# A twelve-layer decoder on one core: softmax sums on TensorE, masking and maximum in one Vector instruction, no copies of the rows

## What is computed

```python
score = jnp.einsum('nqhd,nkhd->nhqk', q, k)
score = jnp.where(mask == 0, jnp.float32(-1e+20), score)
attn = jax.nn.softmax(score / jnp.sqrt(jnp.float32(D)), axis=-1)
out = jnp.einsum('nhqk,nkhd->nqhd', attn, v).reshape(n, lq, H * D)
return out @ Wo.T + bo          # L1x; the others differ in mask, heads and scaling
```

## Time and profile before

| | us |
|---|---|
| median of 3 runs | 3718.55 (3714.80 to 3731.33) |
| the profiled execution, its own time | 3732.82 |
| its span | 3731.0, granted clock 0.905 on average |
| PE busy | 2976.7 (80%) |
| DVE busy | 2299.4 (62%) |
| ACT busy | 1749.1 (47%) |
| POOL busy | 747.6 (20%) |

### The profile page before, as it was taken

The page is one execution under the profiler, slowest core; times in us unless marked ns, Lnnn a source line. Parts: engine busy times, 40 slices in busy tenths (PEclk is TensorE's granted clock), DMA queues, the critical chain, the costliest instruction groups (busy, mean ns, idle before and its releaser), DMA issues. The chain is left out here.

```text
span 3731.0 us, 54776 instructions
## 1 busy us (share of the span) xinstructions
PE 2976.7 (80%) x18517; PEld 2127.6 (57%) x18517; DVE 2299.4 (62%) x5176; ACT 1749.1 (47%) x4238; POOL 747.6 (20%) x865
## 2 busy tenths in 40 slices
PE   6999999998776895676877654595799848888797
PEld 5777777776565583454554324244596435555485
DVE  6777667775566335776777786897311675555423
ACT  6666666665421222776677262403332325555121
POOL 2111111110101421354444000000110003333422
PEclk8999999999898997898899777798799979999799
DMA  3111111111002583000000000000696010000476
GB/s 119 43 46 38 35 35 49 43 35 40 18 1 77 178 294 130 1 1 15 16 7 1 26 0 0 3 0 12 235 343 221 23 49 13 24 24 12 159 257 212
DMA packets 109524, 264.81 MB, mean 71 GB/s; under 512 B 16928, under 2 KB 71456, under 8 KB 104384
## 3 DMA queue, kind: packets, MB, share of 16 engines
q1 hardware_dynamic: 92896, 229.01, 18.4%
q0 software_dynamic: 8688, 23.78, 1.7%
q10 hardware_dynamic: 7664, 8.51, 0.7%
HBM read 213.72 MB, written 47.54 MB: 70 GB/s over the span
## 5 line engine op out<-in xcount | busy, mean ns | idle before, releaser
L1296 POOL TENSOR_TENSOR L3x_p<-L3x_p,L3x_rsum 128x512 f32<-128x512 f32 x128 | 133.0, 1040 | 448.1 <-DVE L3x_rsum L1377 448.1
L3025 POOL TENSOR_TENSOR L0a_sum_sq<-L0a_sum_sq,L0a_sq 128x512 f32<-128x512 f32 x56 | 73.1, 1305 | 698.7 <-ACT L0a_sq L2944 698.7
L2847 ACT ACTIVATE L0a_ex<-bank,L0a_nb 128x128 f32<-128x128 f32 x512 | 145.2, 367 | 126.1 <-PE bank L2776 125.6
L3113 DVE TENSOR_TENSOR L0a_ru<-bank,L0a_um 128x512 f32<-128x512 f32 x128 | 88.2, 689 | 182.1 <-PE bank L2768 167.2
L3104 DVE SCALAR_TENSOR_TENSOR L0a_xf<-L0a_xc,L0a_conv,L0a_xf 128x256 f32<-128x256 f32 x432 | 178.7, 482 | 9.1 <-ACT L0a_xf L2909 7.7
L1358 DVE SCALAR_TENSOR_TENSOR L3x_s<-bank,L3x_bias 128x512 f32<-128x512 f32 x128 | 86.4, 681 | 134.3 <-PE bank L1136 134.3
L1986 PE MATMUL bank<-L2a_half,L2a_diag 128*128 128x512 f32 x328 | 144.1, 601 | 28.4 <-ACT L2a_diag L1969 28.4
L1296 POOL TENSOR_TENSOR L1x_p<-L1x_p,L1x_rsum 128x512 f32<-128x512 f32 x128 | 132.2, 1040 | 138.6 <-DVE L1x_rsum L1377 138.6
L1300 POOL TENSOR_TENSOR L1a_p<-L1a_p,L1a_rsum 128x128 f32<-128x128 f32 (+1 forms) x256 | 123.0, 506 | 137.7 <-DVE L1a_rsum L1377 135.6
L2690 PE MATMUL bank<-x_feat,L0a_wx 128*128 128x256 f32 x576 | 138.1, 391 | 4.1 <-ACT L0a_xc L2896 4.1
L2776 PE MATMUL bank<-L0a_ru,L0a_vm 128*128 128x512 f32 x256 | 137.6, 621 | 0.0
(11 more groups left out here) (727 smaller groups left out, 8215.8 us busy)
## 6 DMA issues: line engine op xcount, KB each, us to landing
L2f_wt<-in_L2f_w SPq DMA_DIRECT2D x23, 2180.0 KB, 10.2
L0f_wt<-in_L0f_w SPq DMA_DIRECT2D x39, 898.0 KB, 6.7
L3f_wt<-in_L3f_w SPq DMA_DIRECT2D x39, 768.0 KB, 5.0
L0a_wx<-in_L0a_wx SPq DMA_DIRECT2D x72, 256.0 KB, 3.1
L0a_wz<-in_L0a_wz SPq DMA_DIRECT2D x32, 512.0 KB, 4.1
context_keys_values<-L2f_zeros ACTq DMA_DIRECT2D x32, 256.0 KB, 4.9
L0f_xs<-rows_by_expert SPq DMA_DIRECT2D x39, 128.5 KB, 3.4
L3f_xs<-rows_by_expert SPq DMA_DIRECT2D x39, 128.5 KB, 2.8
```

The lines of the kernel that those rows point to most:

```text
L1296: last = nc.gpsimd.tensor_tensor(both, both, rsum[r % 2][:, i, :].unsqueeze(2).to_broadcast([P, S, NK]), ALU.mult)
L2847: last = a(ex[g % 3][:, j, b * P:(b + 1) * P], bank[:, at:at + P], ACT.Exp, bias=nb[r % 2][:, b, h:h + 1])
L3113: rv.empty(vec.tensor_tensor(ru[g % 2][:], bank[:].rearrange("p (j t) -> p j t", j=2), um[:].unsqueeze(1).to_broadcast([P, 2, T]), ALU.mult))
```

## The change

1. Twins (L1a, L1x): `exponent` has no running sum any more, `reciprocal` and the division of the probabilities are gone. `weigh` multiplies each transposed tile twice: by the values, and by `summing`, a constant of zeros and ones (128 x 32 for each twin), which gives the sum of the probabilities in every row of the head's features. The accumulator bank now holds the values' product in columns 0 to 255 and the sums in 256 to 511, for one half of the heads, two steps. Every two steps ACT copies the bank to `raw` (`half`), DVE inverts 128 x 256 of it (`inverse`), and POOL multiplies into cT.
2. Masked stages (L1x, L3x, L2x): scale, mask and maximum are one DVE call, `tensor_tensor_reduce`: out = (bank + bias) * -scale, with the running minimum as second output. For L1x two calls (one for each tile of 256), for L3x one of 512, for L2x one of 256. ACT then waits for this alone. L1a keeps its two operations.
3. xb and cb are gone from `softmax_attention`: the projections read `c.xT` and `c.ctxT`. The loop of one turn is gone. L2x keeps its copies.
4. Order, twins: `take_turned` on DVE comes right after the first `scale_mask` of a step; q is projected in step 0 and k in step 1; the output projection comes one step later on PE, and DVE's part of it at the end of that step.

```diff
-        UNITS = [[("k", 0)], [("q", 0)], [("v", 0)], [("v", 1)]]
+        UNITS = [[("q", 0)], [("k", 0)], [("v", 0)], [("v", 1)]]
...
-        xb = [sb(f"xb{i}", [P, KD, T]) for i in range(2)]
-        cb = [sb(f"cb{i}", [P, KD, T]) for i in range(2)] if kind != "latent" else xb
+        raw = [sb(f"raw{i}", [P, 2 * T]) for i in range(2)] if twins == 2 else None
+        summing = sb("summing", [P, 2, DS]) if twins == 2 else None
...
                 def weigh(u):
+                    if twins == 2 and u % 2 == 0 and u:
+                        pe.wait_ge(sig("raw"), u // 2)
...
                     for kt in range(KT):
+                        for of in range(twins):
                             for d in range(G):
...
-                                    at = 0 if causal and kt == 0 else P if causal else 0
-                                    out = acc[0][rows_out, tile * T + at:(tile + 1) * T]
+                                    at = P if causal and kt else 0
+                                    out = acc[0][rows_out, of * T + at:(of + 1) * T]
+                                    weights = summing[:, e, :] if of else weights
...
-                        if step == 0 and r:
+                        if step == twins - 1 and r:
                             output(r - 1)
...
+                def half(i):
+                    act.wait_ge(sig("weighted"), 2 * (i + 1))
+                    if i >= 2:
+                        act.wait_ge(sig("cT"), i - 1)
+                    nc.scalar.activation(raw[i % 2][:], acc[0][:], ACT.Copy).then_inc(sig("raw"), 1)
...
+                def inverse(i):
+                    dve.wait_ge(sig("raw"), i + 1)
+                    below = raw[i % 2][:, T:2 * T]
+                    vec.reciprocal(below, below).then_inc(sig("reciprocal"), 1)
...
+                    for i in range(2 * ROWS):
+                        pool.wait_ge(sig("reciprocal"), i + 1)
+                        if i >= 2:
+                            pool.wait_ge(sig("projected"), i // 2)
+                        nc.gpsimd.tensor_tensor(cT[:, i % 2, :], raw[i % 2][:, 0:T], raw[i % 2][:, T:2 * T], ALU.mult).then_inc(sig("cT"), 1)
...
-                            ins = vec.scalar_tensor_tensor(out=s[:], in0=bank[:, 0:W], scalar=scale,
-                                                           in1=bias[r % 2][:].rearrange("p t s -> p (t s)"), op0=ALU.mult, op1=ALU.add)
+                            ins = vec.tensor_tensor_reduce(out=s[:, at:at + nk], in0=bank[:, at:at + nk], in1=bias[r % 2][:, e, :],
+                                                           scale=-scale, scalar=3e38, op0=ALU.add, op1=ALU.min,
+                                                           accum_out=nmax[r % 2][:, i, e:e + 1])
...
                         if twins == 2:
                             if d == 0 and g < total:
                                 scale_mask(g)
+                            if d == 0 and u > LA:
+                                take_turned((u - LA) * G - 1)
                             if d < G - 1 and g < total:
                                 scale_mask(g + 1)
-                            if d == 1 and u > LA:
-                                take_turned((u - LA) * G - 1)
+                    if twins == 2 and d == G - 2 and u > LA + 2 and (u - LA) % 2 == 1:
+                        inverse((u - LA - 3) // 2)
+                    if twins == 2 and i == G - 1 and r >= 2:
+                        output(r - 2)
...
-                        if g < total:
+                    if causal and g < total:
                         maximum(g)
```

More of the change, by code:

```diff
@@ new lines, in weigh @@
+                                last = nc.tensor.matmul(out, weights, come_from, start=(e == 0 and kt == 0 and of == 0),
+                                                        stop=(e == twins - 1 and kt == KT - 1 and of == twins - 1))
+                    last.then_inc(sig("weighted"), 1)
+                for what, i in in_order:
+                    project(0, what, i)
+                for u in range(-1, steps + LA + 1):
+                    own = range((u - LA) * G, (u - LA + 1) * G) if LA <= u < steps + LA else []
+                    for j in own[:G // 2]:
+                        transposes(j)
+                    if u > LA:
+                        r, step = divmod(u - LA - 1, PER_ROW)
+                        if step == twins - 1 and r:
+                            output(r - 1)
+                        weigh(u - LA - 1)
+                    if 0 <= u < steps:
+                        for r, what, i in units_at(u):
+                            project(r, what, i)
+                    if u + 1 < steps:
+                        r, step = divmod(u + 1, PER_ROW)
+                        if step == 0:
+                            key = ("q", r, MQ // 2 - 1)
+                            pe.wait_ge(t_emptied(key), n_emptied[key])
+                            pe.wait_ge(sig("k_taken"), K_UNITS * (r + 1))
+                            if kind == "latent":
+                                pe.wait_ge(sig(f"kv{r % 2}"), 32 * (r // 2 + 1))
+                        scores(u + 1)
+                    for j in own[G // 2:]:
+                        transposes(j)
@@ L1453, in _ @@
-                    if kind == "latent":
-                        spread(ROWS - 1)
-                    output(ROWS - 1)
-            sig.clear()
-        sig.close()
+                        vec.tensor_tensor(y[:], proj, rowwise(bo), ALU.add).then_inc(sig("out_read"), 1)
+                        dve.wait_ge(sig("out_read"), r + 1)
+                    vec.tensor_tensor(xr, xr, y[:], ALU.add).then_inc(sig("added"), 1)
+                hide(0)
+                for what, i in in_order:
+                    if what == "k":
+                        project(0, i)
@@ L1461, in layer1_attn @@
+                if twins == 2:
+                    inverse(2 * ROWS - 1)
+                if kind == "latent":
+                    spread(ROWS - 1)
+                output(ROWS - 1)
+        sig.clear()
+    sig.close()
 def layer1_attn(c):
```

646 lines of the change are left out of this document (296 added, 350 removed).

## The result

The changed kernel takes 3675.98 us (median of 4 runs, 3673.24 to 3678.78) beside 3724.94 for the kernel before (median of 4); the ratio is 0.9854, with a 95% interval of 0.9829 to 0.9878. The profiled execution takes 3678.78, with a span of 3677.0, 54 us less than the profiled one of before. Forecast was 3686, 33 us less, in a range of 3650 to 3712.

A forecast was written before the change was run, and what follows sets the result against it. PE was taken as nearest the bound in L1a and L1x and bounding L3x, DVE's chain L2x. Terms of -7.5 (L1a), -14.2 (L1x), -3 (L2x), -8 (L3x) gave -33 us: 3686 as median, range 3650 to 3712.

The forecast's parts named there:

- The signs that were named: What would show the forecast: `weigh` and output times, row pitch in L1x, DVE load, PE idle time, stage lengths.
- Sums on PE: L1a and L1x: sum matmuls add to PE's time, +25.3 and +32.0 us.
- Waits for DVE's copy: L1a and L1x: PE's waits for DVE's late copy go by the new order, -29.8 and -37.4 us.
- The waits for cT: L1a and L1x: cT is made a step earlier than needed, so PE's waits go, -5.4 and -4.2 us.
- New waits: L1a and L1x: allowance for PE waiting on DVE behind its large reciprocals, +8 and +4 us.
- The end of a stage: L1a and L1x: nothing covers the last reciprocal and POOL's product, +2.4 us a stage.
- Clock: Twin stages: PE waits less before outputs, so its clock holds better, -7 us in L1a, -10 in L1x.
- Rival (b): Clock holds everywhere, L3x included (-12), and allowances aren't needed (-12): -57 us, 3662; chance 0.15.
- Fused call: L1x on DVE: mask and maximum in one call take 0.50 us, between 0.34 and 0.84; by itself pays nothing there.
- L3x fused: L3x: ACT's exponential, and its copies for PE behind it, start earlier, 0.5 us a row, -4 us.
- L2x fused: L2x: one maximum a row leaves DVE's in-order chain, 8 x 0.34 = -3 us.
- Copies: Removing row copies: ACT's xb no longer delays cT in L3x, -4 us; first projection, -1 in each twin stage.

The follow-up runs named there:

- e7: Changed kernel with the sum products made twice and accumulated: 3726.03 us, ratio to before 0.9998; L1a +20.4, L1x +27.5 us.
- e1: Kernel before with one line moved, DVE's copy right after a step's first scaling in the twin stages: 3703.01 us, ratio to before 0.9897.
- e8: Changed kernel with DVE's copy put back behind the second scaling: 3715.4 us, ratio to before 0.9957; L1a +23.7, L1x +15.4 us.
- e3: Changed kernel with ACT's copy of the accumulator moved ahead of two exponentials: 3676.54 us, ratio to before 0.983; L1x -11.9, L1a -0.8 us.
- e2: e6 plus mask and maximum fused in L1x, L3x and L2x; no sums on TensorE: 3653.26 us, ratio to before 0.9757.
- e6: e1 with the row copies removed, nothing fused: 3651.94 us, ratio to before 0.978.
- e4: Changed kernel with scale, mask and maximum as two DVE instructions again in L3x and L2x: 3714.32 us, ratio to before 0.9917; L3x 398.0 us.
- e5: Changed kernel with ACT's copies of the rows of x put back in L3x alone: 3696.17 us, ratio to before 0.9899; L3x 399.5 us.

## Why the prediction was right, and where its sum was not

The direction, the range and the mechanism hold: order takes PE's holes away, the sums eat a good part of that, and the clock comes back. The sum of the stages was 20 us short (-32.7 against -52.5), 15 of it in L3x. In the twin stages it was 4 short each, and part of that nearness is luck: PE's new waits cost 5 and 8 us more than allowed, the sums 5 and 4.5 less, and the clock gave back more. The signs that were named came so: `weigh` 1.87 us for 2.0, the output's matmuls 1.89 for 2, L1x's rows every 31.48 for 31, DVE in L1x 63% busy, PE's idle time there 28.7 us, a little under the 30 named, and stages of 233, 262, 52 and 371 us for 235, 266, 48 and 384. By its terms:

**Sums on PE**, +25.3 and +32.0, taken at the upper end as the instructions are certain. The second set of e7 costs 20.4 and 27.5: right in that nothing hides them, 5 too much in each. The mis-sized thing is the distance taken as the price, 1.00 us for a `weigh` of 16. In the changed kernel it is 1.87 for 32. In L1a the half-width products are the cheap part: four groups start at 1642.42 and the next instruction at 1643.86, 1.44 us for 32 where 1.58 was taken.

**Waits for DVE's copy**, -29.8 and -37.4. They are gone to 1.4 and nothing; e1 and e8 show that it is the order that does it. The waits for cT, -5.4 and -4.2, are gone in mid-stage too; in L1x they were 3.4 before. The reasoning on places in the queue was right for the new place. It was wrong for the old one, where I counted two scalings and a maximum, and e8 shows three.

**New waits**, +8 and +4, for a DVE that is late behind large reciprocals. This isn't what came. The reciprocal takes 1749 ns as forecast from the earlier trace rows (1742) and no PE wait follows it. What came is 12.7 and 12.2 us for ACT's copy of the accumulator, every second step, which the prediction had at nothing. The change has one bank for values and sums, so `weigh` must wait until ACT has read it, and the copy stood behind four exponentials in a queue whose wait was in plain sight in the diff (`pe.wait_ge(sig("raw"), ...)`). e3 gets it back in L1x. The end of a stage was right in kind: 3.4 us of wait for POOL's last product in each, 2.4 forecast; the product takes 728 ns, not the 613 of the earlier trace rows, and ACT's copy of the bank, 0.58, stands ahead of the chain and was left out.

**Clock**, -7 and -10 in the twin stages, none in L3x. From length and mean clock, low clock loses 289.2 x 0.12 = 34.7 us in L1a before and 278.0 x 0.09 = 25.0 after, in L1x 24.0 and 14.1, in L3x 20.5 and 7.8: -9.7, -9.9 and -12.8. These clocks are rounded to 0.01, which is 3 us of such a stage, and they count idle time too. By PE's busy time for the same instructions, the sums taken at e7's 21.1 and 27.0, it is -12.2, -15.5 and -12.1. So the twins' terms were somewhat small, and L3x's, put at nothing, was the step that failed. Rival (b) had it at -12 with a chance of 0.15, and the reason given against it was that L3x keeps a hole of 1.65 before its output. The hole that is kept is 1.38 us, and the clock falls behind none of the eight outputs.

**Fused call**, taken at 0.50 between 0.34 and 0.84. It is the lower bound, one call every 0.35 us. In the rows of before ACT's read of 193 ns follows an exponential; on DVE the read of 83 ns lies beside the next call. The Trainium skill, VectorE: DVE Perf Modes, section Two Vector instructions with no wait between them, calls such an op two instructions; for an op without a pointer scalar it holds the second, the read, only where its output starts in another quadrant than the last output did. All of these start in the same one, and the two records at 1900.28 agree. The same page of the Trainium skill, section Rules for kernel authors, advises against fusing chained DVE ops for speed. Here the trace disagrees: 0.70 us an item for two calls stand in place of 683 + 667 ns, and e2 against e6 shows 9.2 us of L1x by it. The prediction said that this pays nothing in L1x by itself, and that was false without the sums. PE's waits for DVE's copy and scalings, 3.9 and 2.7 us in e6, are gone in e2, its waits for ACT grow by some 2, and its busy time falls by 5.7. That the clock rose because the waits went is likely, but no run takes the two apart. In the changed kernel the call wasn't undone in L1x, so what it is worth there is open.

**L3x fused**, -4, measured 10.5 between e4 and the changed kernel and 7.0 between e6 and e2, where the clock is the same in both (PE busy 331.9 and 331.5). It makes ACT's copies earlier, as the prediction has it: PE's waits for them are 31.1 us in e4 and 24.6 in the changed kernel. The term was under 60% of the smaller value.

**L2x fused**, -3, measured -0.2. DVE is 6.6 us less busy there, and the time comes back as a wait: the small reciprocal `L2x_rsum` waits 7.3 us for PE (1.4 before). ACT waited for DVE's maximum 3.8 us in all before and 2.4 after, so little of the chain went through it. In one row of the timeline after, DVE's call is done at 2540.04, and ACT's exponential starts at 2541.24, behind two copies; no run tests it further.

**Copies**, -4 in L3x and -1 in each twin stage. e5 has 12.0 in L3x: 3.8 of idle time, as forecast, and 8.2 of PE at low clock, which this term did not have. Alone (e6) they are worth 10.2 in each twin stage. How much of that is left inside the changed kernel, where the output comes a step later anyway, was not tried; nor was the new place of the q and k projections, or the missing loop, by itself.

The account of L1x closes so: PE's idle time falls by 29.5 us (72.5 to 43.0), and its waits give -37.4 (DVE's copy), +12.2 (ACT's accumulator copy), -2.2 (the first projection: 6.6 to 4.4), -1.6 (scores) and -0.9 (the norm's rows). PE's busy time rises by 11.5: 27.0 for the sums (by e7), and 15.5 less for the same instructions as before.

## What to carry to other kernels

Where an engine is near its bound and has holes, look first for what stands ahead of the late copy in another engine's queue; moving one line gave 41 us here, and the added mathematics on the bound engine cost 42 to 60. Before work moves onto the bound engine, ask who waits for the engine that does it now. PE had waited for POOL 0.4 us in L1a and never in L1x, so 27 us of products in L1x replaced divisions that were hidden already. When a change shares a bank between two users, cost the wait for its release by what is queued ahead of the copy that frees it.

## What the runs showed of the hardware that was not expected

- An accumulator's read on DVE (83 ns) starts together with the next call and adds nothing to the pitch of the calls, 0.35 us for 128 x 256 from PSUM.
- A hole ahead of TensorE's output that is 0.51 us longer can be followed by 1.69 us more of matmuls. In L3x, after 1.38 us the 16 matmuls take 3.69 us (granted clock 1.00), after 2.17 us 5.38, and after 1.89 us either, but the last row's output also takes either after 1.27 us (5.38 before and in e4, 3.69 after the change); in L1x of e1 the same hole of 1.40 us is followed by 2.79 to 2.89 us in three rows and by 1.97 in the next two. So the hole alone doesn't set it, and what does is left open.
- POOL's product of two tiles of 128 x 256 takes 728 ns where its product with a broadcast column takes 613.
